# Graph attention layer: VectorE's two scans pulled apart, two PSUM banks for the scores, new orders on TensorE and ScalarE

## What is computed

```
hl = x @ Wl.T + bl;  hr = x @ Wr.T + br
s  = leaky_relu((hl[src] + hr[dst]) * alpha)            # alpha: one 128-vector per edge
e  = exp(s - segment_max(s, dst)[dst])
out = layernorm(x + segment_sum(x[src] * e / segment_sum(e, dst)[dst], dst))
```

## Time and profile before

| | us |
|---|---|
| median of three runs | 1435.29 |
| lowest and highest | 1434.33, 1435.62 |
| span of the profiled execution | 1129.4 |
| median less span | 305.9 |
| busy in the span: PE, PEld, DVE, ACT, POOL | 1079.0, 1014.7, 1072.6, 998.6, 820.7 |

### The profile page before, as it was taken

One profiled execution on the slowest core, in us unless ns is written; L12 is line 12 of the kernel. 1 busy time (PEld: TensorE's weight loads), 2 busy tenths in 40 slices (PEclk: granted clock), 3 DMA queues, 4 the chain that ended last, 5 costly groups with the idle time before them and its releaser, 6 DMA issues.

```text
span 1129.4 us, 34988 instructions
## 1 busy us (share of the span) xinstructions
PE 1079.0 (96%) x9403; PEld 1014.7 (90%) x9403; DVE 1072.6 (95%) x1526; ACT 998.6 (88%) x2606; POOL 820.7 (73%) x858
## 2 busy tenths in 40 slices
PE   6879999999999999999999999999999999999984
PEld 5779999999999999999999999999999899999863
DVE  7889999999999999999999999999999999999967
ACT  4359999999999999999999999999999889998996
POOL 5577777777777777777777777777777777777770
PEclk9889999999999999999999999999999999999997
DMA  9887776666667776767766666677676666676533
GB/s 227 290 221 191 192 187 191 190 188 188 191 187 191 189 189 187 192 189 190 189 189 188 189 191 190 188 189 188 191 189 185 186 188 182 187 191 183 143 99 114
DMA packets 231064, 211.97 MB, mean 188 GB/s; under 512 B 46375, under 2 KB 204286, under 8 KB 230788
## 3 DMA queue, kind: packets, MB, share of 16 engines
q0 software_dynamic: 39872, 108.39, 35.5%
q1 hardware_dynamic: 190442, 100.03, 32.4%
q10 hardware_dynamic: 565, 1.33, 0.4%
HBM read 198.95 MB, written 11.47 MB: 186 GB/s over the span
## 4 chain that ended last, share of the span: by engine, by line
PE 51%; POOL 26%; issue 11%; ACT 3%; DVE 2%; DMA 0%; ACTq 0%; POOLq 0%; DVEq 0%
POOL xg L435 25%; PE ps_w L654 19%; PE ps_sT L590 11%; PE ps_u L630 9%; PE ps_z L608 5%; PE ps_q L599 2%; PE ps_u L636 2%; PE ps_qT L618 2%; ACT attr L853 1%; DVE stats L1161 1%; ACT acc L802 0%; DMA xg<-gather_rows,srcT 0%; ACT right L811 0%; DVE acc L1086 0%; ACT ex L749 0%
## 5 line engine op out<-in xcount | busy, mean ns | idle before, releaser
L435 POOL DMA_INDIRECT xg<-gather_rows,srcT x808 | 764.9, 947 | 253.0 <-issue 235.9
L654 PE MATMUL ps_w<-onehot,ex 128*128 128x128 f32 x3328 | 405.7, 275 | 1.2 <-ACT acc L806 1.2
L654 PEld LDWEIGHTS ps_w<-onehot,ex 128*128 128x128 f32 x3328 | 388.4, 192 | 1.8 <-issue 1.6
L1095 DVE TENSOR_TENSOR_SCAN ps_F<-line,B,ps_sT 128x512 f32<-128x512 bf16 x208 | 266.1, 1279 | 1.0 <-issue 1.0
L1100 DVE TENSOR_TENSOR_SCAN B<-line,ps_F 128x512 f32<-128x512 bf16 x208 | 254.0, 1221 | 7.2
L630 PEld LDWEIGHTS ps_u<-right,onehotT 128*128 128x128 f32 x1664 | 208.5, 192 | 18.9 <-issue 0.2
L630 PE MATMUL ps_u<-right,onehotT 128*128 x1664 | 221.1, 276 | 0.0
L802 ACT ACTIVATE acc<-ps_w 128x768 f32 x208 | 168.7, 811 | 23.5
L1105 DVE TENSOR_TENSOR z<-ps_sT,B 128x512 f32<-128x512 f32 x208 | 143.9, 692 | 7.1
L1121 DVE TENSOR_TENSOR ex<-ps_z,xg 128x512 f32<-128x512 f32 x208 | 141.7, 681 | 5.7 <-ACT ps_z L773 5.7
L1129 DVE TENSOR_TENSOR v<-ps_u,attr 128x512 f32<-128x512 f32 x208 | 141.8, 682 | 0.3
(11 more groups left out here) (264 smaller groups left out, 1164.1 us busy)
## 6 DMA issues: line engine op xcount, KB each, us to landing
attr<-edge_attr_in SPq DMA_DIRECT2D x832, 64.0 KB
line<-step_lines SPq DMA_DIRECT2D x182, 128.0 KB
xg<-gather_rows,srcT POOLq DMA_INDIRECT x808
gather_rows<-acc SPq DMA_DIRECT2D x12, 512.0 KB, 6.0
line<-soon_lines SPq DMA_DIRECT2D x26, 128.0 KB
edge<-step_lines SPq DMA_DIRECT2D x182, 4.0 KB
acc<-x_in SPq DMA_DIRECT2D x6, 448.0 KB, 7.6
xg<-x_in SPq DMA_DIRECT2D x6, 448.0 KB, 5.6
```

The costliest lines, as they stand in the source:

```text
L435: pool.indirect_dma_start(out=xg[:, k % SLOTS, i, :], out_offset=None, in_=rows_dram, in_offset=bass.IndirectOffsetOnAxis(ap=srcT[:, k * W ...
L654: last = nc.tensor.matmul(columns, ex[:, (k - 1) % 2, c, i, :], onehot[:, (k - 1) % 3, i, :], start=(i == 0), stop=(i == WIDE - 1), skip_g ...
L1095: V.tensor_tensor_scan(ps_F[:, :], line[:, k % LINES, 0:GE], ps_sT[:, :], B[:, (k - 1) % 3, GE - 1:GE], ALU.add, ALU.max).then_inc(F_ok, 1)
```

## The change

VectorE's order becomes F(k), add(k+2), B(k), msg(k-1), z(k), v(k+2). `ps_sT` becomes two banks used in turn, and sT(k+1) waits for z(k-1) instead of z(k). The bank comes from `ps_qT`: q and qT share `ps_q`. TensorE's order becomes sT(k+1), zT(k), q(k), u(k+3), first half of w(k-1), qT(k+4), second half of w(k-1). q(k) now waits also for onehotT(k+3), and qT(k+4) for onehot(k). ScalarE's order becomes ex(k), had, gap(k), onehot(k), ez(k), lift(k+2), factor, onehotT(k+4), sums. TensorE still takes the left rows of one chunk in four (L636), as before. No operation is added or taken away.

```diff
-        ps_u, ps_qT = pb("ps_u"), pb("ps_qT")
-        ps_sT = pb("ps_sT")
+        ps_u = pb("ps_u")
+        ps_sT = [pb("ps_sT0"), pb("ps_sT1")]
...
@@ TensorE, body(k)
                     pe.wait_ge(v_ok, k + 2)
-                    if k >= 0:
-                        pe.wait_ge(z_ok, k + 1)
+                    if k >= 1:
+                        pe.wait_ge(z_ok, k)
+                    bank = ps_sT[(k + 1) % 2]
...
                 if has(k):
-                    j = k % EDGES
-                    if k >= 1:
-                        pe.wait_ge(oh_ok, k)
-                    for i in range(WIDE):
-                        last = nc.tensor.matmul(ps_q[:, i * P:(i + 1) * P], edge[:, j, i * P:(i + 1) * P], node[:, :],
-                                                start=(i == 0), stop=(i == WIDE - 1), skip_group_check=True)
-                    last.then_inc(q_ps, 1)
                     pe.wait_ge(z_ok, k + 1)
...
                     last.then_inc(z_ps, 1)
-                if has(k + 4):
...
-                    nc.tensor.matmul(ps_qT[:, :], nodeT[:, :], edge[:, j, :], start=True, stop=True).then_inc(qT_ps, 1)
+                    j = k % EDGES
+                    if k >= 1:
+                        pe.wait_ge(oh_ok, k)
+                    pe.wait_ge(ohT_ok, min(k + 4, STEPS))
+                    for i in range(WIDE):
+                        last = nc.tensor.matmul(ps_q[:, i * P:(i + 1) * P], edge[:, j, i * P:(i + 1) * P], node[:, :],
+                                                start=(i == 0), stop=(i == WIDE - 1), skip_group_check=True)
+                    last.then_inc(q_ps, 1)
                 if has(k + 3):
...
-                    for c in range(2):
+                for c in range(2):
+                    if has(k - 1):
                         for i in range(WIDE):
...
+                    if c == 0 and has(k + 4):
...
+                        if k >= -3:
+                            pe.wait_ge(ohT_ok, k + 4)
+                        if k >= 0:
+                            pe.wait_ge(oh_ok, k + 1)
+                        nc.tensor.matmul(ps_q[:, :], nodeT[:, :], edge[:, j, :], start=True, stop=True).then_inc(qT_ps, 1)
@@ ScalarE, body(k): lift moved from the top to behind ez, onehot ahead of ez
...
+                    act.wait_ge(e_ok, k + 1)
+                    nc.scalar.activation(ps_z[:, :], ps_z[:, :], ACT.Exp).then_inc(e2_ok, 1)
+                if has(k + 2):
+                    act.wait_ge(v_ok, k + 3)
...
@@ VectorE, body(k)
-                    V.tensor_tensor_scan(ps_F[:, :], line[:, k % LINES, 0:GE], ps_sT[:, :],
+                    V.tensor_tensor_scan(ps_F[:, :], line[:, k % LINES, 0:GE], ps_sT[k % 2][:, :],
                                          B[:, (k - 1) % 3, GE - 1:GE], ALU.add, ALU.max).then_inc(F_ok, 1)
-                    dve.wait_ge(F_ok, k + 1)
-                    if k >= 2:
-                        dve.wait_ge(gap_ok, k - 1)
-                    V.tensor_tensor_scan(B[:, k % 3, ::-1], line[:, k % LINES, GE:0:-1], ps_F[:, ::-1], -BIG,
-                                         ALU.add, ALU.max).then_inc(B_ok, 1)
-                    dve.wait_ge(B_ok, k + 1)
-                    if k >= 2:
-                        dve.wait_ge(z_ps, k - 1)
-                    V.tensor_tensor(z[:, k % 2, :], ps_sT[:, :], B[:, k % 3, :], ALU.subtract).then_inc(z_ok, 1)
                 if has(k + 2):
                     j = (k + 2) % SLOTS
                     dve.wait_ge(rows_in[j], 16 * (WIDE - 1) * ((k + 2) // SLOTS + 1))
...
+                if has(k):
+                    dve.wait_ge(F_ok, k + 1)
+                    if k >= 2:
+                        dve.wait_ge(gap_ok, k - 1)
+                    V.tensor_tensor_scan(B[:, k % 3, ::-1], line[:, k % LINES, GE:0:-1], ps_F[:, ::-1], -BIG,
+                                         ALU.add, ALU.max).then_inc(B_ok, 1)
                 if k == STEPS:
                     ratio(0)
                 if has(k - 1):
...
+                if has(k):
+                    dve.wait_ge(B_ok, k + 1)
+                    if k >= 2:
+                        dve.wait_ge(z_ps, k - 1)
+                    V.tensor_tensor(z[:, k % 2, :], ps_sT[k % 2][:, :], B[:, k % 3, :], ALU.subtract).then_inc(z_ok, 1)
                 if has(k + 2):
                     j = (k + 2) % ATTRS
```

More of the change, by code:

```diff
@@ L186, in build_gnn_layer @@
         ps_x = [ps_z, ps_F]
-        ps_left = [ps_sT, ps_u]
+        ps_left = [ps_sT[0], ps_u]
         ps_right = [ps_q[:, :], ps_w[:, 0, :]]
@@ L191, in build_gnn_layer @@
         ps_col = ps_w[:, 1, 400:408]
-        ps_cnt, ps_src = ps_w[:, 1, 0:PR], ps_qT[:, 0:PR]
+        ps_cnt, ps_src = ps_w[:, 1, 0:PR], ps_sT[1][:, 0:PR]
         ps_heads, ps_D = ps_w[:, 0, 0:3 * PR], ps_w[0:PR, 1, 0:P + 2]
-        ps_ahead = [ps_qT[:, :], ps_w[:, 1, :], ps_qT[:, :], ps_w[:, 0, :], ps_w[:, 1, :], ps_w[:, 0, :]]
+        ps_ahead = [ps_sT[1][:, :], ps_w[:, 1, :], ps_sT[1][:, :], ps_w[:, 0, :], ps_w[:, 1, :], ps_w[:, 0, :]]
         ps_t = [ps_z, ps_F]
-        ps_y = [(ps_u[:, :], ps_qT[:, :]), (ps_sT[:, :], ps_q[:, :]),
+        ps_y = [(ps_u[:, :], ps_sT[1][:, :]), (ps_sT[0][:, :], ps_q[:, :]),
                 (ps_z[:, :], ps_F[:, :]), (ps_w[:, 0, :], ps_w[:, 1, :])]
@@ L554, in opening @@
                     pe.wait_ge(v_ok, STEPS)
-                    pe.wait_ge(ohT_ok, STEPS)
+                    pe.wait_ge(z_ok, STEPS)
                 if c == 1:
@@ L589, in body @@
                         for i in range(WIDE):
-                            last = nc.tensor.matmul(ps_sT[:, i * P:(i + 1) * P], part[:, i, :], ident[:, :],
+                            last = nc.tensor.matmul(bank[:, i * P:(i + 1) * P], part[:, i, :], ident[:, :],
                                                     start=(h == 0 and i == 0), stop=(h == 1 and i == WIDE - 1),
@@ L655, in body @@
                                                     start=(i == 0), stop=(i == WIDE - 1), skip_group_check=True)
-                    last.then_inc(sums_ps, 1)
+                        if c == 1:
+                            last.then_inc(sums_ps, 1)
+                    if c == 0 and has(k + 4):
+                        j = (k + 4) % EDGES
+                        if k + 4 < EDGES:
+                            pe.wait_ge(edges_in, 16)
+                        else:
+                            pe.wait_ge(edge_in[j], 16 * ((k + 4) // EDGES))
+                        if k >= -3:
[3 more added lines that the diff above has]
+                        nc.tensor.matmul(ps_q[:, :], nodeT[:, :], edge[:, j, :], start=True, stop=True).then_inc(qT_ps, 1)
                 if k + 4 == SOON:
@@ L737, in body @@
             def body(k):
[L738 to L744, removed]
                 if has(k):
@@ L770, in body @@
                                          bias=B[:, k % 3, 0:1], scale=-1.0).then_inc(gap_ok, 1)
-                    act.wait_ge(e_ok, k + 1)
-                    nc.scalar.activation(ps_z[:, :], ps_z[:, :], ACT.Exp).then_inc(e2_ok, 1)
-                if has(k):
                     act.wait_ge(q_ps, k + 1)
@@ L779, in body @@
                                          bias=1.0, scale=-1.0).then_inc(oh_ok, 1)
+                    act.wait_ge(e_ok, k + 1)
+                    nc.scalar.activation(ps_z[:, :], ps_z[:, :], ACT.Exp).then_inc(e2_ok, 1)
+                if has(k + 2):
+                    act.wait_ge(v_ok, k + 3)
+                    if k >= -1:
+                        act.wait_ge(sT_ps, k + 2)
+                    nc.scalar.activation(lift[:, :, :].rearrange("p i d -> p (i d)"),
+                                         v[:, k % 2, :, :].rearrange("p i d -> p (i d)"), ACT.Relu, scale=SLOPE - 1.0)\
+                        .then_inc(lift_ok, 1)
                 if has(k):
@@ L789, in body @@
                         act.wait_ge(u_ps, k + 3)
-                    nc.scalar.activation(onehotT[:, k % 2, :], ps_qT[:, :], ACT.Relu, bias=1.0, scale=-1.0)\
+                    nc.scalar.activation(onehotT[:, k % 2, :], ps_q[:, :], ACT.Relu, bias=1.0, scale=-1.0)\
                         .then_inc(ohT_ok, 1)
```

## The result

The change made the kernel slower: 1452.55 us (median of four, 1450.01 to 1452.95) against 1435.45 us (four, 1434.33 to 1440.87), a ratio of 1.0118 with a 95% interval of 1.0099 to 1.0136. The prediction was slower by 57 us, to 1492 us with a range of 1465 to 1517: right in sign, but the measured 17 us are less than a third of it and lie outside the range.

What follows compares the result with a forecast made beforehand. VectorE (4.83 us a step) and the gathers (5.006) were taken to bound the kernel. Start 66.7, 207 steps of 5.15, opening 2.4 and end 51.4 gave 1186.6 us of span, 57.2 more, so 1492 us; range 1465 to 1517.

Steps and rivals of the forecast that it cites:

- What bounds the kernel before: VectorE sets the pace at 4.83 us a step until the gathers' lead is used up, then their 5.006 us.
- VectorE's own sum: VectorE's six starts, all independent of the one before, take 4.60 us a step, 0.23 less than before.
- The ring through `ps_u`: v, TensorE's u and the add wait on one bank: add stands 0.55 us, step 5.15 us (5.05 to 5.27).
- the same ring over z: TensorE's zT and q, ahead of u, need z: from z through u and add back to z, 5.21 us.
- The opening: u(3) to u(5) have 16 instructions instead of 10, and a full add: 2.4 us in all.
- The end: Time behind the last forward scan stays the same 51.4 us.
- The sum: Span total 1186.6 us, 57.2 more than 1129.4; added to the median 1435.3, it gives 1492 us.
- rival 3: qT behind onehot, q behind onehotT, or ScalarE's longer route adds a wait: 5.35 us a step, 1533 us; chance 0.06.
- Rivals 1 and 2: Step under 5.0 us: first, gathers rule, 1435 us, chance 0.07; second, also a faster end, 1432 us, chance 0.03.

Runs made afterwards that it cites:

- e5: Kernel before with three gathers a step instead of four from step 10 on, old rows used for the fourth chunk; 1123.16 us, ratio 0.9931.
- e2: Changed kernel with VectorE's add(k+2) put back behind B(k), everything else as changed; 1134.0 us, ratio 1.0026 to the kernel before.
- e4: Changed kernel with L629 doubled, two more TensorE instructions of 0.11 us in u; 1224.08 us, ratio 1.0823.
- e14: Changed kernel without any gathers from step 10 on, old rows used; 1179.62 us.
- e10: Kernel before, unchanged, run with a profile where it was slow (held condition); 1412.97 us.
- e0: Kernel before, unchanged, run again with a profile (quick condition); 1131.56 us, ratio 0.9998 to its other runs.
- e1: Changed kernel, unchanged, run again with a profile (quick condition); 1178.23 us, ratio 1.0407 to the kernel before.
- e3: Changed kernel with VectorE's order of before; banks and TensorE's and ScalarE's orders stay as changed; 1131.86 us, ratio 1.0011.
- e9: Changed kernel with a step's four attribute loads made one of 256 KB from a fixed address, held condition; 1405.28 us, ratio 0.9940.
- e6: Kernel of e2 with three gathers a step instead of four from step 10 on; 1113.84 us, ratio 0.9844.

## Why the prediction was wrong

**What bounds the kernel before: right where its rows were taken.** Two paces, VectorE's 4.84 us and the gathers' 5.006: e5 took one gather away and won 8 us of the 10 expected; e2 shortened VectorE's own step (4.69 us in its shortest steps) and won nothing.

**VectorE's own sum: right as far as it was seen.** B to msg is 1.12 us for a scan of 1.21, so an independent follower starts 0.09 early behind the backward scan too, and the pair that is pulled apart wins 0.12 us (1.26 against 1.14 between starts, in e2). Behind the forward scan no run shows it, since the add there waits for TensorE; the sum of 4.60 us was never reached. The prediction set these rows against the Trainium skill ("VectorE: DVE Perf Modes", section "The DRAIN you can't avoid"). That was half a reading: the section says that the next operation does not start until the pipe is empty, but also that "A next op that is not held starts earlier" (a rule for two VectorE instructions, not the held condition above). The independent followers here, 0.08 to 0.09 us early, agree with the second sentence.

**The ring through `ps_u`: right, in place and size.** 5.15 us forecast, 5.09 measured, the add waits 0.43 us instead of 0.55. The terms that were too large are u (1.38 for 1.42), B to msg (1.12 for 1.14) and msg to z (0.58 for 0.60). Which of the two rings closes it, the one over v or "the same ring over z", is not shown: the rows make them a tie. Over z the terms are z 0.68, to zT's load 0.06, from there to u's load 0.68, u 1.38, 0.11, then 0.47, 1.12 and 0.58, again 5.08 us (5.21 forecast). TensorE's idle time in this stretch lies ahead of zT, which waits for z, and none lies ahead of u, whose loads follow q's at once, while u also starts only 0.14 behind v's end:

```profile
PEld ps_z L602 <- DVE z L1128: 86.6, 208, 3.3
```

The difference matters. The ring over v exists because `ps_u` is one bank. The ring over z does not need it: it exists because u stands behind zT and q in TensorE's order, and a second `ps_u` bank would leave it as it is. e2, e4 and e14 show what the two have in common, u and the add, by giving it slack, lengthening it, and taking the gathers away.

**The opening: right,** 2.4 us forecast; the steps of 5.25 and three times 5.88 us are 2.5 us more than four of 5.09. **The end** was taken as 51.4 us behind the last forward scan and is 54.5.

**The sum failed at its base.** The step that is wrong is "(305.9 us lie outside the span and stay)". In the quick condition the sum gives 1186.6 + 1.8 = 1188 us against 1178 measured, and +57 against +47: the loop with its opening is 13.1 us shorter than forecast, the end 3.1 us longer. But the times on record belong to executions with another step. The changed kernel's was 6.36 us there. In e10 the kernel before has 281 us more span than in e0: 268 us of it in the loop, 1.3 us in each of 207 steps, and 13 us ahead of the first forward scan. No trace of the runs at 1435 us is kept, but by the same measure nearly all of their 306 us lie inside the loop, and only some 1.8 us outside the span.

The difference of 5.15 and 4.84 is not the one that counts there, because another ring, from the gathers over TensorE's held signals back to the gathers, already takes 6.2 us in the kernel before. The held signals add 1.3 us to the step of both kernels, and the 0.25 us of the ring through u do not come on top of that. What is left of the change on record is 17 us, 0.08 us a step. Where they come from is argued, not shown. One candidate: q(k) and u(k+3) now stand behind onehotT(k+3), whose release, qT's signal, is one of the held ones. The page on record has 132.5 us of TensorE's idle time ahead of q, released by onehotT, and e1 has none:

```profile
L609 PE MATMUL ps_q<-node,edge 128*128 128x128 bf16 x832 | 80.4, 219 | 132.5 <-ACT onehotT L794 132.5
```

This is the wait of rival 3, which costs nothing in the quick condition (e3). Another candidate: the held signals come 1.16 us after a step's last gather has ended on record, and 1.02 us in e10. And the kernel before alone differs by 21 us between its two held sets (1435 and 1414 us), more than the 17 us in question. Rivals 1 and 2 needed a step under 5.0 us and did not come about.

**What stays open:** why the gathers hold TensorE's signals in some sets of runs and not in others, whether the matmuls themselves end late, and which wait makes the 17 us. SyncE's transfers are not what holds the signals: they go on in the pauses of e10, and halving them in e9 left the hold as it was. That 306 us was an odd thing to lie outside a span could have been asked before: a base that the profile does not explain belongs in the range.

## What to carry to other kernels

Pulling dependent neighbours apart on a full engine wins 0.12 us a pair between starts here (0.05 us a step in e6), but it can shorten the time that another engine has for its part. Before an operation is moved, walk two kinds of rings: that of every bank that has no partner (last reader, writer, next reader), and that of every engine's order (what stands ahead of the writer, and what that waits for). And before a sum is made, compare the span with the time. Here they differ by 1.8 us wherever both are recorded for one execution; 306 us meant that the profile was of another kind of execution than the times, and the forecast needed a term for that. In a trace of an unexplained condition, look for the steps in which the suspect is absent: here the kernel had three of its own.

## What the runs showed of the hardware that was not expected

- Two conditions of the same program on one core: 1131 us and 1413 to 1435 us, with VectorE's, ScalarE's and GpSimd's operations alike within 2% and a mean granted clock of 0.98 to 0.99 in both. In the held one TensorE's semaphore updates are recorded up to 2.2 us (medians, by operation) after the matmul's modelled end, several within 0.3 us of each other, instead of 0.014 us after each.
- In the held condition the signals of sT and w are late beside gathers and prompt in every step without them (e10: 397 late, 18 prompt). They come 1.02 us after the last gather of a step has ended in e10, and 1.16 us on record.
- On record one in four of SyncE's register moves took 0.7 us instead of 0.03. In e9, with half of SyncE's transfers, no SyncE instruction of the loop took over 0.5 us, and TensorE's signals were held all the same.
- A gather of 128 rows occupies GpSimd for 0.946 to 0.949 us and is followed by 0.305 us of pause, in both kernels and both conditions.
